# First feed-forward stage, feature turns and layer 2's attention joined into one program block

## What is computed

```
h = layer_norm(x, ln_mlp_scale, ln_mlp_offset)            # end of layer 1
x = x + gelu(h @ w_fc1 + b_fc1) @ w_fc2 + b_fc2           # 256 -> 1024 -> 256
q = x @ Wq + bq;  k = ctx @ Wk + bk;  v = ctx @ Wv + bv   # layer 2, 32 heads of 8, 8 key heads
attn = softmax(q k^T * scale + mask)                      # [b, head, 64, 64]
x = layer_norm(attn v @ Wo + bo + x) * gamma + beta
```

## Time and profile before

| | us |
|---|---|
| median of 3 runs (1667.35 to 1671.11) | 1669.09 |
| the profiled execution's own time | 1668.78 |
| its span, first to last instruction | 1667.2 |
| mean granted clock of TensorE | 0.970 |
| busy: PE 1546.1 (93%), DVE 1103.6 (66%), ACT 673.1, POOL 455.6 | |
| feed-forward stage of layer 1, first to last matmul | 1090.8 to 1183.1 |
| feature turns on PE | 1184.1 to 1188.0 |
| layer 2, from its first PE instruction to DVE's last addition | 1189.1 to 1355.1 |

### The profile page before, as it was taken

How to read it: one execution, slowest core, us unless ns; L and a number is a source line. 1 busy time by engine, 2 the same in 40 slices (tenths; PEclk the granted TensorE clock), 3 DMA queues, 4 the chain that set the end, 5 groups by cost and what they waited for, 6 DMA issues and landing times. The chain is left out here.

```text
span 1667.2 us, 33250 instructions
## 1 busy us (share of the span) xinstructions
PE 1546.1 (93%) x13291; PEld 1322.5 (79%) x13291; DVE 1103.6 (66%) x2377; ACT 673.1 (40%) x1270; POOL 455.6 (27%) x533
## 2 busy tenths in 40 slices
PE   4987999999999999999999999889788859999799
PEld 2656888888888888888888888779677747888598
DVE  6886666666666776766666666555499945676444
ACT  4654434343433434333343434432366633554322
POOL 2004120020101212210200201232188866663111
PEclk9998999999999999999999999989899979999799
DMA  4000010010000000000100100000320000000000
GB/s 132 1 0 26 14 39 14 1 39 14 27 13 14 26 14 14 26 14 14 40 14 1 39 26 1 29 20 0 81 60 1 1 1 2 2 2 3 1 26 25
DMA packets 44578, 34.12 MB, mean 20 GB/s; under 512 B 10770, under 2 KB 41496, under 8 KB 44312
## 3 DMA queue, kind: packets, MB, share of 16 engines
q1 hardware_dynamic: 44440, 32.17, 6.7%
HBM read 30.00 MB, written 2.10 MB: 19 GB/s over the span
## 5 line engine op out<-in xcount | busy, mean ns | idle before, releaser
L964 DVE STREAM_TRANSPOSE att_pt<-att_prob 32x256 f32<-32x256 f32 x496 | 215.8, 435 | 6.4
L864 ACT ACTIVATE split_q_sb<-psum,g_cols 128x512 f32<-128x512 f32 x128 | 88.3, 690 | 321.6 <-PE psum L732 321.6
L781 PE MATMUL psum<-att_wo_hi,att_ot_hi 128*128 128x256 f32 x512 | 149.2, 291 | 2.5 <-DVE att_ot_lo L977 1.4
L935 DVE TENSOR_REDUCE att_rmax<-psum 128x6 f32<-128x390 f32 (+1 forms) x96 | 49.2, 513 | 151.3 <-PE psum L694 151.3
L781 PE MATMUL psum<-att_wo_lo,att_ot_hi 128*128 128x256 f32 x512 | 144.6, 282 | 0.0
L781 PE MATMUL psum<-att_wo_hi,att_ot_lo 128*128 128x256 f32 x512 | 144.6, 282 | 0.0
L764 PE MATMUL psum<-att_pt,att_v_sb 128*128 128x128 f32 x1024 | 128.5, 279 | 3.5 <-DVE att_ot_lo L977 3.5
L987 DVE TENSOR_TENSOR g_x_res<-psum,g_x_res 128x256 f32<-128x256 f32 x128 | 54.3, 424 | 114.7 <-PE psum L781 88.3
L764 PEld LDWEIGHTS psum<-att_pt,att_v_sb 128*128 128x128 f32 x1024 | 122.7, 193 | 7.9 <-DVE att_ot_lo L977 3.7
L867 ACT ACTIVATE att_k_sb<-psum,g_cols 128x512 f32<-128x512 f32 x128 | 88.2, 689 | 81.0 <-PE psum L732 81.0
L732 PE MATMUL psum<-split_feat_hi,split_wide_hi 128*128 128x512 f32 x256 | 103.7, 405 | 4.5 <-DVE split_feat_lo L1011 3.3
(11 more groups left out here) (287 smaller groups left out, 3947.6 us busy)
## 6 DMA issues: line engine op xcount, KB each, us to landing
g_ctx_f<-in_L_xattn_wq SPq DMA_DIRECT2D x32, 128.0 KB, 2.2
g_ctx_f<-in_L_xattn_wk SPq DMA_DIRECT2D x32, 128.0 KB, 2.3
g_ctx_f<-in_L_xattn_wv SPq DMA_DIRECT2D x8, 512.0 KB, 3.6
g_ctx_f<-in_L_xattn_wo SPq DMA_DIRECT2D x8, 512.0 KB, 3.8
c_ctx_tok<-in_ctx SPq DMA_DIRECT2D x4, 512.0 KB, 5.5
g_x_res<-in_x SPq DMA_DIRECT2D x4, 512.0 KB, 8.7
g_w<-in_L_xattn_mlp_w SPq DMA_DIRECT2D x2, 1024.0 KB
out<-g_x_res SPq DMA_DIRECT2D x8, 256.0 KB, 2.2
```

The costliest lines, as they stand in the source:

```text
L781: mm = pe.matmul(o_ps[p % 2], a, b, start=(h == 0 and t == 0), stop=(not last and h == HG - 1 and t == 2))
L864: act.activation(q_sb[:, h, :], q_ps[:, :], ACT.Identity, bias=G.cols[:, layer, head:head + 1]).then_inc(q_ready, 1)
L935: dve.tensor_reduce(rmax[:, a:b], s_ps[group][:, :, :], X_AXIS, ALU.max).then_inc(max_done, 1)
L964: turned = dve.transpose(pt[to:to + 32, :, :, r, u, 32 * a:32 * a + 32].rearrange("p h a t -> p (h a) t"), by_pair[of:of + 32, :, u, 32 * ...
```

## The change

- `phase_mlp` for layer 1, `phase_features` and `phase_grouped_attention` become one block, `phase_mlp_grouped_attention`. The hardware loop over blocks 1 to 3 becomes written-out instructions.
- DVE first makes a tile `zero` of 128 x 512; PE waits for it before its first matmul. The four outputs of `down` now lie two to a PSUM bank, and one matmul of 512 columns with `zero` clears each bank (8 in all); DVE adds a bank at a time (8 additions of 512 columns in place of 16 of 256). The freed banks are those of layer 2's projections and contexts.
- Layer 2's preparation moves into block 1 of the stage, the turns of blocks 0 to 2 into blocks 2 and 3, and `project(0)`, `project(1)` and their moves and keys into block 3. `scores(0)` stands before the last two `down`s. The turns of the last block come after `project(2)`.
- SP issues the mask ahead of layer 2's weights, and layer 3's weights after the last `down`. POOL zeroes v_bd and `one` before its first addition, and adds up the context at each second slice, through blocks 0 and 1.
- `pile` lays tensors whose lives don't meet over one another: the activations over layer 1's dead weights, feat_f and pt over the context's halves, soft over feat_hi, and layer 3's weights over all of these weights.
- From step t = 2 on, the orders of layer 2 are as before but for those turns. Layer 3 and its feed-forward stage compute the same from other addresses.

```diff
+def phase_mlp_grouped_attention(nc, A, G, w, b1, g, loads, loads3):
...
             def _(sp):
+                for c in range(2):
+                    sp.dma_start(mask[T * c:T * c + T, :, :],
+                                 A["mask_Bx1xSxS2_ff0"].rearrange("b o q t -> q (b o) t")).then_inc(mask_in, 16)
                 load(nc, sp, loads, arrived)
+                sp.wait_ge(out_psum, 2 * NBLK)
+                load(nc, sp, loads3, late)
...
             def _(pool):
...
                 pool.tensor_tensor(lo_w, raw_w, hi_w.bitcast(F32), ALU.subtract).then_inc(w2_ready[1], 1)
+                pool.memset(v_bd[:, :, :, :, :], 0.0).then_inc(v_zero, 1)
+                pool.memset(one[:, :], 1.0).then_inc(one_made, 1)
...
-                    elif join_context and n % 4 == 1:
+                    elif n < 2 * KT * NBLK:
...
             def _(pe):
+                pe.wait_ge(zero_made, 1)
+                for j in range(NBLK):
+                    for f in range(FT):
+                        up(j, f)
+                        if f >= LAG:
+                            down(j, f - LAG)
+                        if (j, f) == (1, 2):
+                            pe.wait_ge(arrived, 16 * len(loads))
+                            pe.transpose(cols_ps, g.rows[:, :], G.ident[0:4, 0:4]).then_inc(cols_psum, 1)
+                        if (j, f) == (1, 4):
+                            pe.wait_ge(bv_done, 1)
+                            accumulate(bias_ps, [(bv_wide[:, :], g.wo[:, c, :]) for c in range(2)]).then_inc(bias_psum, 1)
+                        if (j, f) == (2, 1):
+                            pe.wait_ge(cols_done, 1)
+                            pe.wait_ge(bias_done, 1)
+                            turn_features(0)
+                        if (j, f) == (2, 4):
+                            turn_features(1)
+                        if (j, f) == (LAST, 2):
+                            turn_features(2)
+                        if (j, f) == (LAST, 4):
+                            pe.wait_ge(w_ready, 1)
+                            project(0)
+                        if (j, f) == (LAST, 6):
+                            project(1)
+                    if j == LAST:
+                        scores(0)
+                    for f in range(FT - LAG, FT):
+                        down(j, f)
+                pe.wait_ge(one_made, 1)
+                for t in range(2, PAIRS + 3):
                     if there(t - 1):
                         scores(t - 1)
                     if there(t):
                         project(t)
+                    if t == 2:
+                        turn_features(LAST)
...
             def _(act):
+                        act.activation(act_raw[f % 2], hid_ps[f % RING], ACT.Gelu, bias=b1[:, f:f + 1]).then_inc(raw_done, 1)
...
...
             def _(dve):
+                dve.tensor_tensor(zero[:, :], w.w2[:, 0:2, :].rearrange("p f d -> p (f d)"), w.w2[:, 0:2, :].rearrange("p f d -> p (f d)"),
+                                  ALU.subtract).then_inc(zero_made, 1)
...
+                        if (j, f) == (1, 0):
+                            dve.wait_ge(arrived, 16 * len(loads))
+                            order_weights(0)
...
+                        if (j, f) == (LAST, 4):
+                            dve.wait_ge(spread_made, 1)
+                            place_keys(0)
+                        if (j, f) == (LAST, 6):
+                            place_keys(1)
+                    if j < LAST:
+                        add_block(j)
+                for t in range(1, PAIRS + 3):
                     if there(t - 1):
                         add_mask(t - 1, 0)
                     if there(t - 2):
                         invert(t - 2, 1)
                     if there(t - 1):
                         add_mask(t - 1, 1)
+                    if t == 1:
+                        add_block(LAST)
```

More of the change, by code:

```diff
@@ L65, in sb, with pile @@
         return self.stack.enter_context(self.nc.sbuf_tensor(f"{self.tag}_{name}", shape, dt))
+    def pile(self, name, *layers):
+        kept = []
+        for layer in layers:
+            with ExitStack() as stack:
+                kept.append([stack.enter_context(self.nc.sbuf_tensor(f"{self.tag}_{n}", shape, dt)) for n, shape, dt in layer])
+        words = max(sum(int(np.prod(shape[1:])) for _, shape, _ in layer) for layer in layers)
+        self.sb(name, [P, words])
+        return kept
     def ps(self, name, shape=(P, 512)):
@@ L424, in _ @@
                 skewed(dve, STEPS, body)
[L428 to L452, removed]
 class Operands:
@@ L1049, in _, with mlp_operands @@
                         turn(j - 1)
-def mlp_operands(m, w1_dram, w2_dram, b2_dram):
+def mlp_operands(G, w1_dram, w2_dram, b2_dram):
     w = Operands()
[L1056 to L1059, removed]
+    w.b2, w.w1, w.w2 = (t[tuple(slice(None) for _ in t.shape)] for t in G.late[5:8])
+    w.loads = [(w.w1, w1_dram.rearrange("(k p) n -> p k n", p=P)),
+               (w.w2, w2_dram.rearrange("(f p) n -> p f n", p=P)),
+               (w.b2, b2_dram.rearrange("(o n) -> o n", o=1).partition_broadcast(P))]
     return w
@@ L1150, in down @@
                     pe.wait_ge(act_ready, FT * j + f + 1)
-                    if split_w2 and first and f % (FT // 2) == 0:
-                        pe.wait_ge(w2_ready[f // (FT // 2)], 1)
                     for p in range(PPB):
@@ L1175, in _ @@
             def _(act):
-                for raw_w, hi_w, _ in halves if split_w2 else ():
-                    act.activation(hi_w, raw_w, ACT.Copy).then_inc(w2_high, 1)
                 def block_of_tokens(j, first):
@@ L1212, in _ @@
                     block_of_tokens(j, False)
-UNITS = 4
-def wait(eng, sem, value):
-    if not (isinstance(value, int) and value <= 0):
-        eng.wait_ge(sem, value)
-MAKE_V, SCORE, EXP, NORMALIZE, TURN, VALUES, OUTPUT, ADD = 3, 2, 3, 4, 5, 6, 7, 7
-def unit_slots(j, front, back):
-    for slot in range(2 * UNITS):
-        def at(lag, slot=slot):
-            ahead, t = divmod(slot - lag, UNITS)
-            return (2 * j + ahead, t, ahead % 2) if (front if ahead >= 0 else back) else None
-        yield slot % UNITS, at
```

729 lines of the change are left out of this document (397 added, 332 removed).

## The result

The change does not pay. Its median is 1670.32 us in 20 runs (1668.58 to 1672.74), that of the kernel before 1667.72 us in 20 runs beside them (1663.12 to 1671.11). The ratio is 1.0018, with a 95% interval of 1.0012 to 1.0024: slower by about 3 us (2.6 between the medians), where 1658.5 was forecast. The profiled execution took 1670.71 us, its span 1668.8.

A forecast was written before the change was run, and what follows sets the result against it. PE bounds the feed-forward stage, DVE layer 2's steady part, with an unfilled stretch between. Gains of 9.7 + 0.7 + 0.2 = 10.6 us take 1668.78 to 1658.2; with the median 0.3 above, 1658.5 us, range 1654 to 1664.5.

The forecast's parts named there:

- What is costed at nothing, and its cover: Feed-forward stage: loop branches, inserted waits, POOL's memsets and denser additions delay nobody, so the sum takes nothing for them.
- the one on the slower side: Stage start: weights land late behind the mask on SP's queue; 1672 us for a landing at 1133; chance 0.02.
- T0 9.7 us earlier relative to the stage's start: T0, DVE's start of `add_mask(0, 0)` in layer 2: 21.4 us of path removed, 11.7 of PE work added, 9.7 earlier.
- Waiting for `zero`, 0.85: Stage start: PE waits while DVE makes the zero tile, 0.85 us paid in full, ends 0.7 and 1.3.
- Projections at the full clock, 1.93 each: Block 3: `project(0)` and `project(1)` take 1.93 us each, 3.85 together, upper end 7.1.
- Rival 1: Feed-forward stage: insertions stall PE or projections miss the full clock's price; about 6 us less gain, 1664.5; chance 0.10.
- The thin place at the start, costed at 0 with 1.3 as upper end: Slice 1's low half: DVE ends at 1099.31, PE wants it at 1099.80; costed at 0, upper end 1.3 us.
- rival 5: Stage start: DVE and POOL lock one port pair, so DVE's cast waits out POOL's addition, 1.3 us; 1659.8; chance 0.05.
- The loop's branches at nothing, the loads in time: Block boundaries: the queue's lead hides branches of about 0.2 us; weights land at 1108 to 1112, slice (1, 0) due near 1116.
- Behind T0 0.9 us gained: Layer 2's start: first sum at T0 + 6.2 instead of T0 + 6.96, gain 0.7 us, plus 0.2 for scores at fuller clock.
- from T0 + 7 on DVE has the same work in the same order: Layer 2 behind the first sum: DVE's work and order are unchanged, so nothing further is added to the gain.
- fall into their idle time: Near T0 + 8: the last feature turns, 1 us of PE and 1.2 of ACT, fall where those engines are idle.

The follow-up runs named there:

- after_128: The changed kernel with an unused 128-byte tensor behind the weights' pile, so context and features begin at 128 modulo 256: 1660.83 us, ratio to before 0.9955.
- sets_late: The changed kernel with POOL's two memsets moved from the start of the feed-forward program to slice (2, 1): 1666.60 us, ratio to before 0.9991.
- probe_32: The changed kernel with 128-byte gap, late memsets, later `zero` wait, earlier last feature turn, and features and output weights tiles at 160 modulo 256: 1658.31 us, one run.

## Why the prediction was wrong

**The step that failed** is "What is costed at nothing, and its cover". It goes through the loop, the waits, the memsets and the additions, and leaves out the part of the change that `pile` is: other addresses, which the sum so took at nothing, without a word. Everything ahead of the stage's first matmul was taken as unchanged. But `pile` also moved layer 1's weights further down in SBUF and context and features further up, and layer 1's attention lost 8.1 us by that, three quarters of the whole forecast gain; after_128, with nothing changed but addresses, gets it back. No rival had it: the one on the slower side looked for a late weight load, which did not happen. The range of 1654 to 1664.5 held no value for anything outside the rewritten stretch.

With 128 bytes between the weights and the context, the change as proposed takes 1660.83 us, in the range and 2.3 above the forecast. By its steps:

- **T0 9.7 us earlier relative to the stage's start.** Measured 7.8, and 110.9 - 100.3 = 10.6 with the memsets out of the way (sets_late). The sum of PE's work was right: 10.4 us were added (1205.53 - 1100.38 - 2.46, less the 92.3 of before), where the terms behind the wait for `zero` gave 10.8.
- **Waiting for `zero`, 0.85.** PE's first matmul starts 1100.38 - 1099.61 = 0.77 us after ACT's first operation, against 0.02 before: 0.75.
- **Projections at the full clock, 1.93 each.** 1.89. Rival 1's dear projections and its stalls at (1, 0), (3, 4) and (3, 6) did not appear: the granted clock is 1.00 from 1180 to 1205.5, and PE is busy without a gap from the first clearing matmul to 1205.53.
- **The thin place at the start, costed at 0 with 1.3 as upper end.** Mis-sized: 2.46 us of idle time, 2.7 regained by sets_late. I had looked at slice 1, because it was thin before; but POOL's memsets stand before its first addition, so they and the denser joinings meet DVE in slice 0. The mechanism was rival 5's. The Trainium skill (SBUF — State Buffer, section SBUF: two separate sides) says that the loser of the port pair blocks for the whole instruction. The trace agrees, and here DVE lost three times in a row: its low half from 1105.38 to 1108.63 spans POOL's addition, joining and second addition, 1105.45 to 1108.08, and the 0.07 us before and 0.55 after them make 0.62, near the 0.69 that it takes alone. In sets_late DVE gets in between two of them: the low half ends 0.55 us after POOL's addition, and the joining takes 1.74 us in place of 1.25. What decides who goes next isn't shown; by the recorded starts DVE began first here, by 0.07 us.
- **The loop's branches at nothing, the loads in time.** Both held: no wait of DVE or PE for loads at (1, 0) or (1, 2), and PE has no gap at a block boundary in either trace. That the gapless window contradicts the rule cited there goes too far: no row shows that this loop's target lay outside the fetched pages, so the window shows only that this loop did not stall.
- **Behind T0 0.9 us gained.** The first sum was right (5.97 for 6.2). It carries to pair 1, whose first mask addition starts at T0 + 7.39 (8.38 before), and is gone at pair 2, T0 + 17.50 (17.58 before). That "from T0 + 7 on DVE has the same work in the same order" did not keep it, and that the last turns "fall into their idle time" was wrong: ACT's moves of the last features hold up the first turn of probabilities, PE is at the low clock, and DVE waits 1.62 us for scores(2). From T0 to the start of layer 2's last addition it is 0.7 us more in place of 0.9 less. The gain is missing; that it is a loss isn't settled, since kernels with the same order of work differ there as much: 151.9 to 153.9 us in before and its two variants, 153.1 to 154.0 in after and the six variants that keep its order there.
- **Not foreseen, and its cause open:** about 1.8 us of low clock in layer 1's last outputs. These outputs take 9.1 us after, 7.3 before and 7.3 in after_128. The profiles of before and its two variants have 7.3 us there; of those of after and its ten variants, nine have 9.0 to 9.3, and after_128 and probe_32 have 7.3. That split speaks against mere scatter between executions, but one profile of each kernel doesn't settle it, and no run looks for what in the change would bring it.

## What to carry to other kernels

When a change moves tensors in SBUF, compare the addresses of the operands of every hot matmul before and after, modulo 256 bytes, even in stages whose code it leaves alone; an unused tensor of 32 words ahead of the moved ones told here whether the layout was to blame, with one of 64 words as control. Read an unchanged stage's length in both traces first: here it held most of the surprise. And put an idle engine's preparatory work where the engine that it shares a port with has slack, not at the start of a pipeline, where the first result is waited for.

## What the runs showed of the hardware

- A 512-column matmul of float32 halves starts every 226 to 227 ns or every 228 to 241 ns after the last, at the same full clock (1.00), by where its operands and its neighbours' lie. The fast state looks like a lock: in layer 1 of the kernel before, the six q matmuls after the outputs start 230, 236, 228, 233, 231 and 226 ns apart, and from then on it is 227, 227, 226 to the end of the group. In the kernel after no k matmul of layer 1 is less than 228 ns ahead of the next one. For 256 columns the mean was anywhere from 113.8 to 119.9 ns.
- A DVE cast of 128 x 512 took 1.28 us beside a POOL memset and 0.43 without it; the subtraction behind it 3.25 beside three POOL instructions in a row, 1.11 beside two, and 0.69 alone.
- The granted clock at one moment decides 1 to 2 us. Pair 2's mask addition was 16.1 or 17.9 us behind T0 in two kernels with the same order of work, at 1.00 and at 0.50 of the clock.
